# Queries and keys of two attention blocks from high and low parts: three reduced-precision products in place of one full one, with a re-placed schedule

## What is computed

```python
# block 0: 32 groups, 4 heads of 32 channels
xn = group_norm(x) * scale + bias
q, k, v = Wq.T @ xn + bq, Wk.T @ xn + bk, Wv.T @ xn + bv      # per pixel
p = softmax(q.T k / sqrt(128))                                # per head, 1024 x 1024
x = (x + Wp.T @ (v p) + bp) / sqrt(2)
# block 1: 8 groups, one head of 128 channels, same steps
x = x + proj(softmax(q.T k / sqrt(128)) v) + proj_b
```

## Time and profile before

| | us |
|---|---|
| median of 3 runs | 1655.61 (1654.03 to 1656.54) |
| the profiled execution's own time | 1653.08 |
| its span, from first to last instruction | 1651.3 |
| DVE busy in the span | 1159.9 (70%) |
| ACT busy | 1068.6 (65%) |
| POOL busy | 1120.6 (68%) |

### The profile page before, as it was taken

One profiled execution on the slowest core, in us unless ns is written; L12 is line 12 of the kernel. 1 busy time (PEld: TensorE's weight loads), 2 busy tenths in 40 slices (PEclk: granted clock), 3 DMA queues, 4 the chain that ended last, 5 costly groups with the idle time before them and its releaser, 6 DMA issues.

```text
span 1651.3 us, 25703 instructions
## 1 busy us (share of the span) xinstructions
PE 1598.8 (97%) x9399; PEld 1071.2 (65%) x9399; DVE 1159.9 (70%) x1961; ACT 1068.6 (65%) x1826; POOL 1120.6 (68%) x531
## 2 busy tenths in 40 slices
PE   7898999999999999999999999999999999999988
PEld 5333566666676766667676676766666666676667
DVE  6676676777767777776777777677777767766342
ACT  1454666766676666667666676766667676666744
POOL 2487767876766777676687767678676667868700
PEclk8899999999999999999999999999999999999999
DMA  7404032040412314141130414114041411400000
GB/s 208 122 20 121 20 97 52 33 126 29 128 39 81 68 33 116 39 129 39 68 80 33 116 39 128 34 58 96 21 128 39 124 31 39 109 20 8 7 7 20
DMA packets 47660, 111.69 MB, mean 68 GB/s; under 512 B 5808, under 2 KB 6448, under 8 KB 47536
## 3 DMA queue, kind: packets, MB, share of 16 engines
q1 hardware_dynamic: 47248, 109.86, 23.8%
q10 hardware_dynamic: 288, 0.20, 0.0%
HBM read 67.84 MB, written 41.94 MB: 66 GB/s over the span
## 4 chain that ended last, share of the span: by engine, by line
PE 89%; DVE 5%; ACT 3%; DMA 2%; issue 1%; SPq 0%; POOL 0%; ACTq 0%; POOLq 0%
PE bank L938 14%; PE acc L863 14%; PE scores L906 14%; PE scores L845 14%; PE scores L893 7%; PE bank L947 4%; PE scores L885 3%; PE acc L943 3%; DVE halfmax L724 3%; PE scores L886 3%; PE scores L887 3%; PE bank L943 3%; PE bank L969 2%; PE bank L965 2%; ACT turned L579 1%
## 5 line engine op out<-in xcount | busy, mean ns | idle before, releaser
L518 POOL TENSOR_TENSOR sum<-sum,probs 128x1024 f32<-128x1024 f32 x444 | 1040.1, 2373 | 372.1 <-PE acc L863 372.1
L724 DVE TENSOR_REDUCE halfmax<-bank 128x1 f32<-128x512 f32 x1007 | 666.8, 685 | 232.6 <-PE bank L938 228.9
L559 ACT ACTIVATE probs<-scores 128x512 f32<-128x512 f32 x896 | 515.9, 598 | 186.8 <-PE scores L845 183.2
L845 PE MATMUL scores<-q_stack,k_stack 97*128 97x512 f32 x1024 | 447.9, 454 | 2.4 <-DMA q_stack<-neg 2.3
L938 PE MATMUL bank<-k_stack,q_stack 96*128 96x512 f32 x992 | 422.7, 444 | 19.1 <-DVE halfmax L724 8.6
L938 PEld LDWEIGHTS bank<-k_stack,q_stack 96*128 96x128 f32 x992 | 187.0, 191 | 139.9 <-DVE halfmax L724 75.4
L906 PEld LDWEIGHTS scores<-v,turned 128*128 128x128 f32 x1952 | 252.3, 191 | 38.7 <-ACT turned L579 19.2
L906 PE MATMUL scores<-v,turned 128*128 128x128 f32 x1952 | 259.5, 276 | 4.3 <-ACT turned L579 3.8
L845 PEld LDWEIGHTS scores<-q_stack,k_stack 97*128 97x128 f32 x1024 | 194.2, 191 | 98.0 <-issue 79.6
L572 ACT ACTIVATE probs<-scores,negmax 128x1024 f32<-128x1024 f32 x128 | 142.6, 1114 | 157.9 <-DVE negmax L763 157.9
L863 PE MATMUL acc<-probs,v 128*32 128x512 f32 x1792 | 221.9, 607 | 0.0
(11 more groups left out here) (102 smaller groups left out, 1376.4 us busy)
## 6 DMA issues: line engine op xcount, KB each, us to landing
q_stack<-parts_dram SPq DMA_DIRECT2D x96, 256.0 KB, 5.2
k_stack<-parts_dram SPq DMA_DIRECT2D x96, 256.0 KB, 7.0
xin<-x_dram SPq DMA_DIRECT2D x16, 512.0 KB, 3.5
parts_dram<-q_hi SPq DMA_DIRECT2D x16, 512.0 KB, 2.6
parts_dram<-q_lo SPq DMA_DIRECT2D x16, 512.0 KB, 3.1
parts_dram<-k_hi SPq DMA_DIRECT2D x16, 512.0 KB, 3.7
parts_dram<-k_lo SPq DMA_DIRECT2D x16, 512.0 KB, 4.1
x<-x_dram SPq DMA_DIRECT2D x16, 512.0 KB, 3.5
```

The source lines that it names most:

```text
L518: pool.tensor_tensor(total, total, probs[:, ring_slot(i, half, kt), 2 * two:2 * two + 2, :], ALU.add).then_inc(added[two], 1)
L559: act.activation(dst, score_bank(i, index), ACT.Exp).then_inc(exp_done, 1)
L724: dve.tensor_reduce(halfmax[:, h, t, half:half + 1], banks[p][:, :], AX.X, ALU.max).then_inc(bank_free[p][VE], 1)
L845: pe.matmul(score_bank(i, index), ks[0:SPLIT + 1, i % 2, h, tile(kt)], qs[0:SPLIT + 1, q_half(i, half), h, :], start=True, stop=True).then ...
```

## The change

For block 0 of images 1 to 15 and block 1 of images 0 to 14 (`in_parts`), the eight query and key products of a round are each made as three float32r products that add up in the bank: high weight by high image, high weight by low image, low weight by high image. The other pieces (block 0 of image 0, in the head, and block 1 of image 15, in the last round) stay as they were; the value products still read `xh`.

Added for each such image and block: on ACT `high_norm` (`hi0`, `hi1`), the same activation as `norm` once more, with float32r output `xh_hi`; on DVE `low_norm` (`lo0`, `lo1`), `xh_lo = xh - xh_hi`, both operands in SBUF. PE waits for `xh_lo`. The next load of the input tile also waits for `hi0`. Before the head ACT rounds four weights and DVE subtracts. Three small buffers are dropped and their content kept elsewhere. Most pieces have new gaps. Cut to its core:

```diff
-            ("exp1", t, 0, None, first + 1, None),
-            ("rinv", t, 0, None, None, first + 3),
+            ("exp1", t, 0, None, first + 2 - t % 2, None),
+            ("rinv", t, 0, None, None, first + 3 + 2 * (t % 2)),
...
 MAX_EARLY = (
-    19, 25, 27, 27, 28, 35, 36, 36, 38, 43, 44, 47, 51, 53, 53, 57, 59, 60, 64, 65, 66, 67, 67, 68, 69, 71, 76, 77,
-    78, 81, 82, 83, 86, 87,
+    19, 20, 25, 26, 27, 28, 30, 31, 31, 32, 33, 34, 35, 36, 42, 43, 44, 46, 47, 51, 52, 53, 55, 57, 59, 60, 63, 65,
+    66, 68, 69, 74, 75, 76, 78, 81,
 )
 MAX_LATE = (
-    19, 24, 25, 28, 29, 30, 31, 31, 33, 34, 41, 44, 45, 47, 48, 50, 51, 54, 55, 59, 60, 62, 62, 67, 68, 69, 73, 73,
-    74, 79,
+    24, 27, 29, 35, 37, 43, 48, 48, 50, 53, 55, 59, 60, 62, 63, 65, 66, 67, 68, 69, 70, 73, 76, 79, 81, 82, 85, 86,
 )
...
-    ("stats0", 0, 2, None, None, 40), ("mean0", 0, 2, 46, None, 46), ("var0", 0, 2, 49, None, 49),
-    ("affine0", 0, 2, None, None, 61), ("norm0", 0, 2, None, GAPS + 1, None),
-    ("q0", 0, 2, GAPS + 5, GAPS + 5, GAPS + 5), ("q0", 1, 2, GAPS + 5, GAPS + 5, GAPS + 5),
+    ("stats0", 0, 2, None, None, 41),
+    ("mean0", 0, 2, 46, None, 46),
+    ("var0", 0, 2, 52, None, 52),
+    ("affine0", 0, 2, None, None, 59),
+    ("norm0", 0, 2, None, GAPS + 0, None),
+    ("hi0", 0, 2, None, GAPS + 0, None),
+    ("lo0", 0, 2, None, None, GAPS + 3),
+    ("q0", 0, 2, GAPS + 5, GAPS + 5, GAPS + 5),
+    ("q0", 1, 2, GAPS + 6, GAPS + 6, GAPS + 6),
...
+    ("affine1", 0, 0, None, None, GAPS + 25),
+    ("norm1", 0, 0, None, GAPS + 32, None),
+    ("hi1", 0, 0, None, GAPS + 32, None),
+    ("lo1", 0, 0, None, None, GAPS + 35),
+    ("q1", 0, 0, GAPS + 36, GAPS + 36, GAPS + 37),
...
 ADD_THEN = {
-    2: (("scale", 1, -1),), 4: (("form", 0, 0),), 6: (("rstd", 1, -1),), 20: (("rstd", 0, 2), ("scale", 0, 0),),
+    2: (("scale", 1, -1),),
+    6: (("rstd", 1, -1),),
+    7: (("form", 0, 0),),
+    18: (("rstd", 0, 2),),
+    20: (("scale", 0, 0),),
 }
...
+            def high_norm(b, i):
...
+                act.activation(xh_hi[:, :], src, ACT.Identity, bias=gn[b][:, OFFSET:OFFSET + 1],
+                               scale=gn[b][:, GAIN:GAIN + 1]).then_inc(xh_high_done[b], 1)
...
+            act.wait_ge(prep_ve, 4)
+            for n in range(4):
+                act.copy(w_hi[:, n, :], weight_of(n)).then_inc(w_high_done, 1)
...
+                dve.tensor_tensor(xh_lo[:, :], xh[:, :], xh_hi[:, :].bitcast(F32),
+                                  ALU.subtract).then_inc(xh_low_done[b], 1)
...
-                    pe.wait_ge(norm_done[b], i + 1)
-                    weight = wq_scaled[:, b, :] if name[0] == "q" else w(b, WK)
-                    mm = pe.matmul(dst[:, :], weight, xh[:, halves(arg)], start=True, stop=True)
+                    n = 2 * b + (name[0] == "k")
+                    if in_parts(b, i):
+                        pe.wait_ge(w_low_done, 4)
+                        pe.wait_ge(xh_low_done[b], parts_before(b, i) + 1)
+                        pe.matmul(dst[:, :], w_hi[:, n, :], xh_hi[:, halves(arg)], start=True, stop=False)
+                        pe.matmul(dst[:, :], w_hi[:, n, :], xh_lo[:, halves(arg)], start=False, stop=False)
+                        mm = pe.matmul(dst[:, :], w_lo[:, n, :], xh_hi[:, halves(arg)], start=False, stop=True)
+                    else:
+                        pe.wait_ge(norm_done[b], i + 1)
+                        mm = pe.matmul(dst[:, :], weight_of(n), xh[:, halves(arg)], start=True, stop=True)
```

More of the change, by code:

```diff
@@ L64 @@
 BLOCK1 = [(p[0], p[1], -1) + p[3:] for t in range(KT) for p in tile_pieces(t, TILE_FIRST + TILE_GAPS * t)] + [
-    ("out", 0, -1, GAPS + 13, None, GAPS + 13), ("out", 1, -1, GAPS + 42, None, GAPS + 43),
+    ("out", 0, -1, GAPS + 13, None, GAPS + 13),
+    ("out", 1, -1, GAPS + 42, None, GAPS + 43),
 ]
@@ L83 @@
 SHIFTS = [
-    ("gather", 0, 1, None, None, 55), ("shift", 0, 1, 58, None, 58), ("gather", 1, 1, None, None, GAPS + 24),
+    ("gather", 0, 1, None, None, 55),
+    ("shift", 0, 1, 58, None, 59),
+    ("gather", 1, 1, None, None, GAPS + 24),
     ("shift", 1, 1, GAPS + 28, None, GAPS + 28),
@@ L88 @@
 NEXT0 = [
-    ("stats0", 0, 2, None, None, 40), ("mean0", 0, 2, 46, None, 46), ("var0", 0, 2, 49, None, 49),
-    ("affine0", 0, 2, None, None, 61), ("norm0", 0, 2, None, GAPS + 1, None),
-    ("q0", 0, 2, GAPS + 5, GAPS + 5, GAPS + 5), ("q0", 1, 2, GAPS + 5, GAPS + 5, GAPS + 5),
-    ("k0", 0, 2, GAPS + 6, GAPS + 6, GAPS + 8), ("k0", 1, 2, GAPS + 7, GAPS + 7, GAPS + 8),
-    ("v0", 0, 2, GAPS + 11, GAPS + 11, None), ("v0", 1, 2, GAPS + 20, GAPS + 20, None),
+    ("stats0", 0, 2, None, None, 41),
@@ new lines @@
+    ("mean0", 0, 2, 46, None, 46),
[6 more added lines that the diff above has]
+    ("q0", 1, 2, GAPS + 6, GAPS + 6, GAPS + 6),
+    ("k0", 0, 2, GAPS + 6, GAPS + 6, GAPS + 8),
+    ("k0", 1, 2, GAPS + 7, GAPS + 7, GAPS + 8),
+    ("v0", 0, 2, GAPS + 11, GAPS + 11, None),
+    ("v0", 1, 2, GAPS + 20, GAPS + 20, None),
@@ L94 @@
 ]
 CHAIN = [
[L96 to L106, removed]
+    ("save", 0, 0, None, 34, None),
@@ new lines @@
+    ("sums", 0, 0, 45, 45, None),
+    ("recip", (0, 0), 0, None, None, 51),
+    ("recip", (0, 1), 0, None, None, 52),
+    ("recip", (0, 2), 0, None, None, 54),
+    ("recip", (0, 3), 0, None, None, 57),
+    ("proj", 0, 0, 60, None, 62),
+    ("stats1", 0, 0, None, None, 62),
+    ("save", 1, 0, None, GAPS + 3, None),
+    ("sums", 1, 0, GAPS + 7, GAPS + 7, None),
+    ("recip", (1, 0), 0, None, None, GAPS + 10),
+    ("recip", (1, 1), 0, None, None, GAPS + 11),
+    ("recip", (1, 2), 0, None, None, GAPS + 14),
@@ new lines @@
+    ("recip", (1, 3), 0, None, None, GAPS + 15),
+    ("proj", 1, 0, GAPS + 19, None, GAPS + 19),
+    ("stats1", 1, 0, None, None, GAPS + 19),
+    ("mean1", 0, 0, GAPS + 22, None, GAPS + 22),
+    ("var1", 0, 0, GAPS + 23, None, GAPS + 24),
+    ("affine1", 0, 0, None, None, GAPS + 25),
[3 more added lines that the diff above has]
+    ("q1", 0, 0, GAPS + 36, GAPS + 36, GAPS + 37),
+    ("q1", 1, 0, GAPS + 36, GAPS + 36, GAPS + 38),
@@ L107 @@
+    ("k1", 0, 0, GAPS + 38, GAPS + 38, GAPS + 38),
+    ("k1", 1, 0, GAPS + 38, GAPS + 38, GAPS + 39),
+    ("v1", 0, 0, GAPS + 40, GAPS + 41, None),
     ("v1", 1, 0, GAPS + 41, GAPS + 41, None),
@@ L270, in bass_two_attention_blocks @@
         consts = sb("consts", [C, 3, C])
-        wq_scaled = sb("wq_scaled", [C, 2, C])
         bq_scaled = sb("bq_scaled", [C, 2])
         wp_scaled = sb("wp_scaled", [C, C])
-        wv_turned = sb("wv_turned", [C, C])
-        wv_proj = sb("wv_proj", [C, C])
         proj_bias = sb("proj_bias", [C, 2])
@@ L281, in bass_two_attention_blocks @@
         xh = sb("xh", [C, N])
+        xh_hi, xh_lo = (sb(n, [C, N], F32R) for n in ("xh_hi", "xh_lo"))
+        w_hi, w_lo = (sb(n, [C, 4, C], F32R) for n in ("w_hi", "w_lo"))
         part = [sb(n, [C, N], F32R) for n in ("q_hi", "q_lo", "k_hi", "k_lo")]
@@ L330, in bass_two_attention_blocks @@
         norm_done = [sem(f"norm_done{b}") for b in range(2)]
+        xh_high_done = [sem(f"xh_high_done{b}") for b in range(2)]
+        xh_low_done = [sem(f"xh_low_done{b}") for b in range(2)]
+        w_high_done = sem("w_high_done")
+        w_low_done = sem("w_low_done")
         hi_done = [sem(f"hi_done{b}") for b in range(2)]
@@ L397, in turned_of, with in_parts, parts_before, parts_user_before @@
             return probs[:, 0, 2:4, :].rearrange("p h n -> p (h n)") if tile_set(j, t) else turned[:, :]
+        def in_parts(b, i):
+            return i > 0 if b == 0 else i < images - 1
+        def parts_before(b, i):
+            return i - 1 if b == 0 else i
+        def parts_user_before(b, i):
+            if b == 0:
+                return ("k1", 1, i - 3) if i >= 3 else ("k0", 1, i - 1) if i == 2 else None
+            return ("k0", 1, i + 2) if has0(i + 2) else ("k1", 1, i - 1)
+        def weight_of(n):
+            return w(n // 2, WQ) if n % 2 == 0 else w(n // 2, WK)
         def has0(i):
@@ L411, in load_x @@
                 sp.wait_ge(norm_done[0], i)
+                if i > 1:
+                    sp.wait_ge(xh_high_done[0], i - 1)
                 sp.dma_start(xin[:, :], x_dram[i]).then_inc(xin_loaded, 16)
@@ L601, in norm @@
                                scale=gn[b][:, GAIN:GAIN + 1]).then_inc(norm_done[b], 1)
+            def high_norm(b, i):
+                before = parts_user_before(b, i)
+                if before:
+                    act.wait_ge(bank_full[bank_of(before)], filled(before))
+                act.wait_ge(affine_done[b], i + 1)
+                src = xin[:, :] if b == 0 else x1[:, i % 3, :]
+                act.activation(xh_hi[:, :], src, ACT.Identity, bias=gn[b][:, OFFSET:OFFSET + 1],
+                               scale=gn[b][:, GAIN:GAIN + 1]).then_inc(xh_high_done[b], 1)
             def high(b, which, half, i):
@@ L659, in _ @@
                             norm(int(name[-1]), img)
+                        elif name in ("hi0", "hi1"):
```

(30 more changed lines are left out.)

## The result

The changed kernel takes 1768.05 us (median of 4 runs, 1766.72 to 1769.83) against 1655.63 before: ratio 1.0685, 95% interval 1.0671 to 1.0699. It is slower by 112 us where 18 us of gain were forecast. The time lies above every case of the prediction; the mechanism stands among the rivals (A), with a price several times too small.

The account below looks back on a forecast made before the run. PE's work was taken to bound the kernel: 1653.08 - 19.2 (products) + 1.6 (placing) = 1635.5 us, with 2.5 more a median of 1638.0. Forecast 1632 to 1645 (chance 0.50); 8-in-10 range 1624 to 1657.

Parts of the forecast that it names:

- rival A: DVE's subtraction and POOL's additions exclude each other at lo0, lo1: one place 18 us, 1656, chance 0.16; both 1671, 0.10.
- PE's bound: In a steady round of 97.00 us PE is busy 96.57, so its work sets the time.
- the products: On PE, three float32r products replace one float32 piece: 0.16 us saved each, 120 pieces, 1.28 us a round.
- the placing: New gaps for most pieces: gain bounded at 0.9 us a round, none taken; 0.1 a round added, 1.6 in all.
- the head: Four ACT copies and four DVE subtractions before the rounds fit into waits of 7.18 and 4.22 us: nothing.
- the 19.2: PE's whole saving in us from the float32r products: 120 pieces x 0.16.
- POOL's wait for the variance: At block 0's root, moved to after addition 18: 2.3 us, hidden by the 3.07 us wait for the reciprocals.
- the term of DVE's subtraction: 30 low_norm of 128 x 1024 on DVE at 1.22 us each, bounds 1.2 to 1.4 if alone.
- The slack of 1.3 to 1.8 us: Room on DVE at lo0 and lo1 before q0 and q1, if the subtraction takes what it takes alone.
- The phase: Where lo0 and lo1 meet POOL's additions: lo1 waits 1.05 us, covered by slack; lo0 nothing or 2.3 us.
- Rival A with both places: Exclusion hits lo0 and lo1 fully: 15 x 2.2 = 33 us, 1671, slower than before; chance 0.10.
- 0.74 for faster: Chance that the whole kernel ends faster, at 1652.3 us or below; same 0.11, slower 0.15.

Follow-up runs that it names:

- the one-operand run: Changed kernel, but DVE makes xh_lo by a one-operand reduction that copies xh, in place of the two-operand subtraction: 1632.81 us, ratio 0.9861.
- the new places alone: Changed kernel with its new gaps, but all queries and keys as single float32 products, no high and low parts: 1654.21 us, ratio 0.9986.
- the runs with gaps: Changed kernel, POOL waiting for its own last addition: at each addition 1647.21 us; only after additions 12 and 25 1684.22; after 11 and 24 1676.64.
- the twelve probes: One-operand copy kernel plus one 128 x 4 DVE subtraction, both operands in SBUF, in each of rounds 3 to 14: 1660.02 us, single run.

## Why the prediction was wrong

**The frame held.** PE's bound, the products, the placing and the head came as worked out. The three products stand 0.68 us from start to start (879.75 to 880.43) for 0.69 forecast. Where DVE is not kept waiting (the one-operand run, which leaves the subtraction out) the kernel takes 1632.8 us, inside the forecast's 1632 to 1645, and with the subtraction done and POOL pausing 1639.1, 1.1 from the 1638.0. The saving by the difference of two runs, 21.4 us, is a little over the 19.2. By steady rounds it is closer: 97.0 us before, mostly 96.7 to 96.8 with the new places alone, mostly 95.4 to 95.5 in the one-operand run, so the products save 1.3 a round, as worked out, and the new places some 0.25, which was not counted. The subtraction alone takes 1.21 us for 1.22. `high_norm` costs nothing that shows. POOL's wait for the variance is 2.60 us in a round of the one-operand run for 2.3 forecast, and its wait for the reciprocals has fallen from 3.07 to 0.34: it is hidden, as worked out.

**The step that failed is the term of DVE's subtraction** (1.22 us taken, 4.76 measured in the mean), and with it the price of rival A. The slack of 1.3 to 1.8 us at each place was taken "as long as the subtraction takes what it takes alone", and the rival bounded the wait at "the addition in progress, 0 to 2.34 us". The wait was 2.7 to 4.3 us in the steady rounds (3.94 and 5.48 less 1.2). The earlier trace rows had what was needed for the upper bound: POOL's seven additions are printed as one unbroken piece of 16.39 us, and a wait for the end of such a piece would have been bounded by its remainder: from 713.1 to 717.80 at `lo0`, 4.7 us; from 762.0 to 764.29 at `lo1`, 2.3 (measured: 4.3 and 2.7). I bounded it by one instruction because the rule that I had spoke of one.

The Trainium skill, page SBUF — State Buffer, section "Who interferes with whom", says that such a pair excludes each other and the second blocks until the first is done. By that rule rival A was certain in kind, and it was. For the length the trace of the changed kernel disagrees: each of the 29 waited past at least one end of an addition, the longest (6.80 us) past two. Here the measurement decides. In the runs with gaps, and for ten of the twelve probes, the wait mostly ended with the addition in progress, as the page has it. That a reduction with one operand is free of all this (1209 ns) agrees with the same section.

**The phase.** The rival thought of `lo1` as covered and of `lo0` as a matter of luck. With waits to the end of the run neither was: 29 of 30 were hit; only the first, before POOL's additions begin, was not.

**What followed was also too small.** The rival passed 1.0 to 1.3 us of 2.3 on to PE, per place. In the changed kernel 1.77 of 2.7 reach PE at `lo1`, and 3.85 of 4.3 at `lo0`. At `lo0` the slack was 0.4 us, not 1.3: it had been read from DVE's idle time before `q_lo`, but the banks of the maxima, named in the prediction as queued behind, give out before `q0` is due. And then PE's clock is at its lower level for a while, which costs some 3 us a round by the granted clock, which no case of the prediction priced. PE had no rest of this length in a round before, so no row there showed it.

**The chances.** Rival A with both places had 0.10 and 1671 as its end. The range could not hold 1768, since the mechanism's own length was bounded wrongly; 0.74 for faster rested on the same slack.

**What stays open** is who decides at the end of an addition. The runs show that DVE is shut out to the end of an unbroken run in all steady rounds of the changed kernel, that it is let in at the end of an addition where a gap of 0.17 us stands, and that soon behind a gap it is also let in at an end without idle time. What the two engines compare, and from when, was not settled; that it depends on how long POOL has worked without idle time fits all subtractions here but was not tested, and the two long probes, in the fifth instruction, show that it is not all.

## What to carry to other kernels

Before moving work to DVE, count its operands in SBUF: while POOL runs a chain of additions, an instruction with two of them cannot be priced by its own duration. Bound its wait by the time to the end of the chain, whatever its size; it can be as short as the addition in progress, but do not count on it late in a chain. Give it a place where POOL waits anyway, make POOL wait for it (here 1768 to 1639 us), or give it one operand. And price a stall on PE with the clock behind it: stalls of 3.85 us went with 3.4 to 6.8 us at half the clock, in which each matmul took nearly twice as long.

## What the runs showed of the hardware that I had not expected

A DVE subtraction of 128 x 4, through in 0.16 us where it is let in at once, took 9.35 us beside POOL's additions in two cases of twelve, while the additions kept their 2.38. A semaphore wait of POOL on its own last instruction, which costs 0.17 us, brings the subtraction of 128 x 1024 from 4.76 to 2.07 us in the mean; then it is POOL that waits, 0.8 us in one addition.
